# First attention of a fused two-layer kernel: the causal cut of the scores by key goes from a mask product on TensorE to GpSimd

## What is computed

```
q, k, v = lora(x, Wq..), lora(x, Wk..), lora(x, Wv..)      # 16 heads of 16
s = einsum('bhqd,bhkd->bhqk', q, k) / sqrt(16)
s = s + slopes * (i - j) + triu(-inf, 1)                   # mask: key behind query
p = softmax(s);  o = einsum('bhqk,bhkd->bhqd', p, v);  x = x + o @ Wp.T
```

## Time and profile before

| | us |
|---|---|
| median of 3 runs | 2213.62 (2212.52 to 2216.26) |
| the profiled execution | 2214.61 |
| its span | 2212.4 |
| first attention, from the span's start to its last output product | about 595 |
| one batch of it in steady state | 70.0 |

### The profile page before, as it was taken

The page is one execution under the profiler, slowest core; times in us unless marked ns, Lnnn a source line. Parts: engine busy times, 40 slices in busy tenths (PEclk is TensorE's granted clock), DMA queues, the critical chain, the costliest instruction groups (busy, mean ns, idle before and its releaser), DMA issues. The chain is left out here.

```text
span 2212.4 us, 51581 instructions
## 1 busy us (share of the span) xinstructions
PE 1902.9 (86%) x18502; PEld 1350.5 (61%) x18502; DVE 1768.9 (80%) x3807; ACT 1318.1 (60%) x2553; POOL 1000.5 (45%) x1191
## 2 busy tenths in 40 slices
PE   6989998989852999468699989898999999779999
PEld 4666666666551666245467767676666767646665
DVE  8888888888782664578789797989889887779997
ACT  4666666666562454356567676777767686734443
POOL 5443453435014000388767575765757576012222
PEclk8999999999856999799899999999999999989999
DMA  7000000000043333212200000000000000010000
GB/s 253 1 2 2 2 2 1 2 1 2 3 171 106 112 87 108 57 25 44 42 18 21 18 18 18 21 21 18 21 16 23 16 23 17 20 40 17 19 17 24
DMA packets 76581, 79.06 MB, mean 36 GB/s; under 512 B 17248, under 2 KB 68528, under 8 KB 76224
## 3 DMA queue, kind: packets, MB, share of 16 engines
q1 hardware_dynamic: 69728, 66.91, 10.0%
q0 software_dynamic: 6416, 8.95, 2.0%
q10 hardware_dynamic: 208, 0.11, 0.0%
HBM read 38.39 MB, written 20.77 MB: 27 GB/s over the span
## 5 line engine op out<-in xcount | busy, mean ns | idle before, releaser
L379 PE MATMUL a_bank<-w_in_sb,xnT_sb 128*128 128x512 f16 x1152 | 290.8, 390 | 39.2 <-DVE yT_sb L611 21.1
L442 ACT ACTIVATE prob_sb<-a_bank,neg_max_sb 128x128 f32<-128x128 f32 (+3 forms) x512 | 257.2, 533 | 67.2 <-DVE neg_max_sb L546 53.7
L1243 DVE TENSOR_REDUCE neg_max_sb<-a_bank 128x1 f32<-128x128 f32 (+3 forms) x512 | 235.2, 483 | 77.1 <-PE a_bank L972 73.0
L546 DVE TENSOR_REDUCE neg_max_sb<-a_bank 128x1 f32<-128x128 f32 (+3 forms) x512 | 235.6, 480 | 69.0 <-PE a_bank L297 68.9
L1132 ACT ACTIVATE probT_sb<-a_bank 128x512 f32<-128x512 f32 (+1 forms) x384 | 198.7, 526 | 136.4 <-PE a_bank L995 131.4
L450 ACT ACTIVATE p_hi_sb<-a_bank 128x384 f16<-128x384 f32 (+1 forms) x384 | 202.1, 526 | 122.3 <-PE a_bank L306 120.7
L553 DVE TENSOR_TENSOR p_lo_sb<-a_bank,p_hi_sb 128x384 f16<-128x384 f32 (+1 forms) x384 | 226.8, 592 | 40.3 <-ACT p_hi_sb L450 39.8
L306 PE MATMUL a_bank<-ident_f_sb,prob_sb 128*128 128x128 f32 x1280 | 207.8, 277 | 3.9 <-DVE p_lo_sb L553 2.7
L734 POOL TENSOR_TENSOR rope_w_sb<-t_buf_sb,sin_sb 128x256 f32<-128x256 f32 x128 | 145.9, 1140 | 142.9 <-DVE t_buf_sb L594 134.5
L379 PEld LDWEIGHTS a_bank<-w_in_sb,xnT_sb 128*128 128x128 f16 x1152 | 102.8, 100 | 150.3 <-DVE yT_sb L611 27.4
L292 PE MATMUL a_bank<-stack_sb 128*128 128x128 f16 (+3 forms) x512 | 149.6, 305 | 46.6 <-ACT prob_sb L442 22.5
(11 more groups left out here) (246 smaller groups left out, 5550.6 us busy)
## 6 DMA issues: line engine op xcount, KB each, us to landing
stack_sb<-stack_sb SPq DMA_DIRECT2D x256, 64.0 KB
sorted_rows<-zeros_sb SPq DMA_DIRECT2D x1, 4992.0 KB, 22.1
x_in_sb<-sorted_rows SPq DMA_DIRECT2D x39, 128.0 KB, 2.5
sorted_results<-y_moe_sb SPq DMA_DIRECT2D x39, 128.0 KB, 1.7
x_sb_sb<-L_attn_x SPq DMA_DIRECT2D x8, 512.0 KB, 9.9
w_raw_sb<-L_ffn_gate_bank SPq DMA_DIRECT2D x8, 512.0 KB, 3.7
w_raw_sb<-L_ffn_up_bank SPq DMA_DIRECT2D x8, 512.0 KB, 4.6
w_raw_sb<-L_ffn_down_bank SPq DMA_DIRECT2D x8, 512.0 KB, 5.7
```

Source lines behind the costliest of these rows:

```text
L379: last = pe.matmul(out, xnT[:, x, c, j * P:(j + 1) * P], w["in"][:, w_, c, cols], start=k == 0, stop=k == len(terms) - 1)
L442: last = act.activation(prob[g][:, off:off + L], S[(3 * h + g) % 2][:, off:off + L], ACT.Exp, bias=neg_max[:, i:i + 1])
L546: last = dve.tensor_reduce(neg_max[:, i:i + 1], S[(3 * h + g) % 2][:, off:off + L], AX.X, ALU.max, negate=True)
L1243: last = dve.tensor_reduce(neg_max[:, h % 2, i:i + 1], S[(3 * h + g) % 2][:, off:off + L], AX.X, ALU.max, negate=True)
```

## The change

The product L995 is gone from `scores_by_key`; `scores` (by query) keeps its own. The exponentials behind the diagonal are now those of unmasked scores, and POOL overwrites them with zero in `probT`, in a new function `cut`: one affine_select per group, so 48 a batch and 384 in all, on a block of 128x128 (r = 0 and 2) or 128x2x128 (r = 1) of f32. It waits for ACT's `exp` of the same slot; the value products wait for it (`s_cut`) in place of `exp`. In POOL's `slot` the cut stands ahead of `take`, and the takes stay at their slots and keep all their copies. The parts of the value products go from slots 17, 20, 23 to 19, 22, 25, and with them `AT_OUT`, `AT_OT` and the second of `AT_YT` by two. The semaphore `s_zeros` is folded into `s_const`, with the counts raised by one.

```diff
-AT0 = ((1, 4, 7, 10), (13, 16, 19, 22), (24, 27, 30, 33), (31, 34, 37, 40), (17, 20, 23), 24, 26, (63, 66), (73, 76, 91, 94))
+AT0 = ((1, 4, 7, 10), (13, 16, 19, 22), (24, 27, 30, 33), (31, 34, 37, 40), (19, 22, 25), 26, 28, (63, 68), (73, 76, 91, 94))
...
-                pe.matmul(out, stack[0:K0, h % 4, T + kt * P:T + (kt + 1) * P], stack[0:K0, h % 4, kt * P:T],
-                          start=True, stop=False)
-                last = pe.matmul(out[:, 0:P], mask[:, :], ident_b[:, :], start=False, stop=True)
+                last = pe.matmul(out, stack[0:K0, h % 4, T + kt * P:T + (kt + 1) * P], stack[0:K0, h % 4, kt * P:T],
+                                 start=True, stop=True)
...
-            wait(pe, s_exp, 12 * Q + 10 + part)
+            wait(pe, s_cut, 12 * Q + 10 + part)
...
+        def cut(b, h, r):
+
+            wait(pool, s_exp, b * GROUPS + 3 * h + r + 1)
+            t = probT[:, (h // 4) % 2, h % 4, :]
+            at_ = [KT_AT[kt] for kt in KT_GROUPS[r]]
+            if len(at_) == 2:
+                n = at_[1] - at_[0]
+                block_ = t[:, at_[0]:at_[0] + 2 * n].rearrange("p (k n) -> p k n", k=2)[:, :, 0:P]
+            else:
+                block_ = t[:, at_[0]:at_[0] + P].unsqueeze(1)
+            pool.affine_select(block_, block_, [[0, len(at_)], [1, P]], ALU.is_ge, 0.0, base=0,
+                               channel_multiplier=-1).then_inc(s_cut, 1)
...
         def slot(cur, off, k, last):
             b = cur + off
+            if 0 <= k - LAG_S < GROUPS:
+                cut(b, (k - LAG_S) // 3, (k - LAG_S) % 3)
             for kind, ahead, *a in work(k - LAG_WV, last):
```

More of the change, by code:

```diff
@@ L845, in attention0 @@
     s_exp = sem("probsT_ready")
+    s_cut = sem("probsT_masked")
     s_pv = sem("quad_pv_ready")
@@ L882, in attention0 @@
     s_first_k = sem("first_piece_keys_staged")
-    s_zeros, s_padded = sem("zeros_set"), sem("padding_zeroed")
+    s_padded = sem("padding_zeroed")
     bn, mv, sd, rstd = (stats[k] for k in ("bn", "mv", "sd", "rstd"))
@@ L901, in _ @@
             load_expert(sp, d, raw["ring"], raw["loaded"], e)
-        sp.wait_ge(s_zeros, 1)
+        sp.wait_ge(s_const, 1)
         sp.dma_start(xs.rearrange("(s p) n -> p s n", p=P),
@@ L1101, in prologue @@
             pe.wait_ge(s_small, 64)
-            pe.wait_ge(s_const, 2)
+            pe.wait_ge(s_const, 3)
             pe.wait_ge(s_first_k, PIECES)
@@ L1465, in prologue @@
         def prologue():
-            pool.memset(zeros[:, :], 0.0).then_inc(s_zeros, 1)
+            pool.memset(zeros[:, :], 0.0).then_inc(s_const, 1)
             for dst, src in ((al_q[:, :, :, :], d["alibi_q"].rearrange("(t p) h n -> p t h n", p=P)),
@@ L1473, in prologue @@
             pool.memset(one[:, :], 1.0).then_inc(s_const, 1)
-            pool.wait_ge(s_const, 1)
+            pool.wait_ge(s_const, 2)
             pool.wait_ge(s_alibi, 32)
```

## The result

The changed kernel takes 2242.4 us (median of 4 runs, 2238.18 to 2247.49) against 2214.94 for the kernel before (4 runs, 2212.52 to 2220.97): a ratio of 1.0115, with a 95% interval from 1.009 to 1.0139. It is slower by 27 us. I had forecast slower, by 10.5 us: 2224, in a range from 2206 to 2263. The side and the range were right; the size was less than half of what came. All the main terms of the sum were off, one of them by all of its size: the moved value products and turns, which I had at nothing.

The account below looks back on a forecast made before the run. PE and DVE were taken as nearly full, POOL half empty but waited for at each batch change. Cuts +27.2, products -17.2 and a last cut +0.5 gave +10.5 us: 2224.1 us against the median, range 2206 to 2263.

Parts of the forecast that it names:

- What bounds the kernel: First attention: PE and DVE nearly full, POOL half empty, yet PE waits for POOL's copies at each batch change, 4.3 us.
- The products removed: PE's stream: 512 mask products of 0.06 us; three quarters of 22.9 us kept outside slots 32 to 45, -17.2 us.
- The cuts on POOL: 384 selects at 0.40 and 0.61 us (row L1430); nine between takes delay slot 45's fill by 3.9 us, +27.2 us.
- my own sum for the gate: Slot 45's fill behind POOL's takes: +18.6 us over seven batches if cuts cost the lower end, bf16 copy prices.
- my own sign of being wrong: POOL's selects: the forecast is wrong if a cut costs a third of a microsecond or less.
- The gate in slot 19: First value products of a batch, waiting for slot 15's cut: POOL 22.4 us against PE 22.5, level, costed at nothing.
- at slot 17 it would be late by some 3 us: First value products at their old slot: without the two slots of delay the awaited cut would come some 3 us late.
- The rest: Prologue semaphore counts and moved turns cost nothing; DVE's slowdown sits inside the lost quarter; last batch's cut adds +0.5 us.
- The drag on DVE: DVE's L1254 takes 0.42 us with POOL busy, 0.18 idle; a third more time busy, 1.3 us of DVE a batch.
- The clock rival: End of each batch: PE's stall lowers the granted clock, 4 us in seven places, +28 us more, 2252 us; chance 0.08.
- DVE holding the pace: First attention: none of PE's gain is kept, +27.7 us, 2241 us; upper end of the forecast's range, no separate chance.
- Cheap cuts: POOL's cuts at lower-end price, all 22.9 us of PE's gain, fewer DVE waits: -8.8 us, 2204.8 us; chance 0.18.

Follow-up runs that it names:

- f_none_old: Kernel before without the mask product in the scores by key and without cuts, old slots (17, 20, 23): 2197.76 us, ratio 0.9911.
- g_cut_three_early: Changed kernel with the move by three, next rows' turns and first four pieces three slots earlier, second output product in slot 40: 2198.42 us, ratio 0.9935.
- h_cut_double: Changed kernel with each cut made twice, the second behind the first, same values: 2316.79 us, ratio 1.0451.
- f_none_new: Kernel before without mask product and without cuts, value products and turns moved by two as in the change: 2219.73 us, ratio 1.003.
- f_mask_new: Kernel before with only the value products and turns moved by two; mask products kept, no cuts: 2231.66 us, ratio 1.0072.
- h_mask_new_proj: Kernel before with the move by two and the second output product one slot later; mask products kept, no cuts: 2225.13 us, ratio 1.0038.
- g_mask_three: Kernel before with value products and turns moved by three slots; mask products kept, no cuts: 2220.63 us, ratio 1.0048.
- h_mask_three_early: Kernel before with the move by three, rows' turns and first pieces three slots earlier, second output product in slot 40; mask products, no cuts: 2209.56 us, ratio 0.997.
- f_cut_old: Changed kernel with value products and turns back at their old slots (17, 20, 23, 24, 26): 2246.68 us, ratio 1.0136.
- g_cut_three: Changed kernel with the move by three slots in place of two: 2232.62 us, ratio 1.009.
- g_cut_new_early: Changed kernel at its own slots, with rows' turns and first four pieces three slots earlier, an output product moved away: 2231.68 us, ratio 1.0082.
- h_cut_new_proj: Changed kernel with the second output product one slot later: 2233.21 us, ratio 1.0074.

## Why the prediction was right, and where it was wrong

**What bounds the kernel.** Right. PE and DVE full, POOL half empty, and one place in a batch where POOL is waited for the earlier trace rows. Of the cuts' cost that isn't the clock, 2.1 us a batch lie there and 0.3 in the slots 18 to 20, and with the move by three 4 us more for POOL took them away.

**The products removed.** Forecast -17.2 us, three quarters of 22.9; measured -15.1 at the old slots and -12.0 at the new. The step holds, and so does next to nothing being kept at the end of the batch (0.3 us of 1.7 in f_none_old); the share of the 22.9 kept was rather a half to two thirds.

**The cuts on POOL.** Mis-sized: I took L1430's 0.40 and 0.61 us, and they took 0.294 and 0.408, the lower end. "Two things to look at for each element" was no reason to take a row with two inputs from memory; the index isn't one. Its slope of 1.67 ns was also read between an f32 and a bf16 row. With the measured price my own sum for the gate was +18.6 us, and at 0.332 us on average a cut lies on my own sign of being wrong, a third of a microsecond. The cuts cost 20.6 to 22.7 in the runs. In the profiled execution it is 3.9 us a batch: 2.1 at the end of the batch (14.7 in seven), 1.5 by the clock, the rest in the slots 18 to 20. POOL's share in a steady batch is 60% (45.3 of 75.3 us), not 75 to 80: the cuts are cheaper, and before the change it was 41% from 60 to 590 us.

**The gate in slot 19.** Right. I had it level and at nothing: slots 18 to 20 take 4.76 us with cuts and 4.46 without. With each cut doubled it opens, by 4.7 us a batch. But "at slot 17 it would be late by some 3 us" was wrong: at the old slots the value products wait 40.6 us in all, in the slots 41 and 5 and not in 17. Those two gates I hadn't looked at.

**The rest.** This is the step that failed: "the moved turns cost nothing: nobody waits for them today". Together with the value products, whose move I had priced only by what it buys, they cost 18.8 us. I asked who waits for the old ones, and had to ask who waits for the new ones: which bank each fill now takes, whose reader it then waits for, and what else stands in its slot. The list of fills by slot says it at a glance, and the order in front of the prediction even shows it: in slot 31 a piece's product (L1043) ahead of the value products, with a wait for the y of the moved turn (`quad_y_ready`). That is where the move costs 1.8 us a batch. No rival had it either.

The drag on DVE that I had added there didn't come either: L1254 takes 0.215 us on average from 60 to 560 us, and 0.234 before, though POOL is busy for longer. My 0.42 was the top of what L1254 takes beside POOL: in the timeline of before it is 0.294 on average beside POOL's copies and 0.178 with POOL idle. The selects don't leave DVE alone either: beside a cut and nothing else it takes 0.309 in the changed kernel (7 times), 0.241 in g_cut_three_early (25) and 0.269 in h_cut_double (48). The mean fell since L1254 met POOL's copies less often and at less cost.

**The clock rival.** Given 0.08, and it came, beside the forecast rather than in its place. I had priced it at 4 us each in seven places, 28 us. It came in nine, at 1.3 to 1.6 us each where its cost can be read and at nothing ahead of a wait, some 10 us in all. "The stall is short and PE works on both sides of it" was wrong as a reason against it.

**The other rivals.** DVE holding the pace (2241) lies beside the measured time by accident: its mechanism, no gain from the products, is refuted by f_none_old. Cheap cuts came as a price but didn't make the kernel faster, since the move ate them. The forecast of 2224 is short by 18 us: 18.8 of the move and 5.2 of the products, less 5 to 7 of the cuts, in which the clock made up for part of the lower price. Without the move the parts would be -12.0 and +22.7, +10.7 us, next to my +10.5. That is luck: a dear cut without the clock stood in for a cheap one with it. That the time fell into the range is owed to its width.

## What to carry to other kernels

A wait moved to a later slot isn't free because nothing waits there now: write down, slot by slot, what each shared buffer holds before and after, and keep the remainder of the slot when the schedule has a period. Work given to a half-empty engine costs what its longest unbroken row is late by, so give that row more lead: here, together with a move that keeps the slots apart, it turned +1.2% into -0.7% with the same cuts, and neither of the two did it alone. Look at the clock batch by batch, since averages over the stage hide the falls. Price an instruction that the trace doesn't have by its inputs from memory and its width; here that row would have been right.

## What the runs showed of the hardware

An affine_select of f32 on GpSimd, in place, takes 0.294 us for 128 columns and 0.408 for two blocks of 128, as long as a bf16 copy of as many columns (0.297 and 0.403). A DVE subtraction of 4 columns with two inputs in SBUF takes 0.178 us with GpSimd idle and 0.24 to 0.31 on average beside such a select.

The granted clock falls for a few microseconds at a time in an attention stage whose PE is busy for 84% (445.66 of 530 us): 0.58 over 3 us behind 1.54 busy of 3, with no single wait of PE above 1.53 us in the 6 us before. What tips it stays open: f_none_new is thinner still at the same place, 1.47 busy of 3, and has no fall there.

```profile
426.00:429.00 3.00, 1.47 (x19) 1.04 (x17) 2.86 (x10) 1.03 (x3) 0.00 (x0) 1.00 0.00 0
429.00:432.00 3.00, 2.17 (x22) 1.03 (x20) 1.70 (x4) 1.91 (x4) 0.00 (x0) 1.00 0.00 0
```

Over the kernels here the clock sum goes with PE's waits for the cuts and with the crowding. It is 0 to 3.4 us in the kernels without cuts, crowded (f_mask_new, f_none_new, h_mask_new_proj) or not (before, f_none_old, g_mask_three, h_mask_three_early), and in g_cut_three_early, which has all the cuts and next to no wait for them. It is 12 to 25.6 us in those with cuts and waits for them (after, f_cut_old, g_cut_three, g_cut_new_early, h_cut_new_proj), and 54.6 in h_cut_double. That cuts alone, without a wait of PE, would do it isn't shown. Each sum is of one execution.
